# First batch of a four-batch transformer kernel: a second set of buffers for every other chunk, and another order of loads and set-up

## The reference, cut to what matters

```python
x = x + attn0(ln(x))   # one head, key and value size 64, causal, biases on q, k, v and the output
x = x + ffn0(ln(x))    # ln(x) and the weight clipped to +-448 and rounded to fp8 e4m3, product in fp16, + bias
x = x + attn1(ln(x))   # 16 heads of size 16, rotary embedding on q and k, causal
x = x + ffn1(ln(x))    # xr, xk mix a row with the row before it; sigmoid(xr Wr) * (relu(xk Wk)^2 Wv)
```

## Time and profile before

| what | us |
|---|---|
| median of 3 runs | 2985.44 |
| lowest and highest | 2980.69 to 2988.47 |
| the profiled execution's own time | 2989.6 |
| its span in the trace | 2987.8 |
| granted TensorE clock, mean over the span | 0.953 |
| PE busy in the span | 2646.4 (89%) |
| DVE, ACT, POOL busy | 2008.9, 1570.6, 400.0 |

### The profile page before, as it was taken

One profiled execution on the slowest core, in us unless ns is written; L12 is line 12 of the kernel. 1 busy time (PEld: TensorE's weight loads), 2 busy tenths in 40 slices (PEclk: granted clock), 3 DMA queues, 4 the chain that ended last, 5 costly groups with the idle time before them and its releaser, 6 DMA issues.

```text
span 2987.8 us, 57907 instructions
## 1 busy us (share of the span) xinstructions
PE 2646.4 (89%) x21682; PEld 1189.2 (40%) x21682; DVE 2008.9 (67%) x4383; ACT 1570.6 (53%) x3137; POOL 400.0 (13%) x417
## 2 busy tenths in 40 slices
PE   3677869989989999999999989999989999999996
PEld 2333333343434434343344434434334443443344
DVE  3435567778684776867675677777667668778822
ACT  1133325656563565655554555655555556666662
POOL 2212102020200302021010202102020110000011
PEclk8788879999999999999999999999999999999998
DMA  2332123131220313113130221313021131121110
GB/s 53 91 98 79 30 64 86 30 88 35 56 80 29 99 34 93 51 44 93 30 92 29 64 82 44 99 34 98 16 76 53 38 107 33 48 58 28 31 33 30
DMA packets 239508, 176.06 MB, mean 59 GB/s; under 512 B 89793, under 2 KB 238978, under 8 KB 239234
## 3 DMA queue, kind: packets, MB, share of 16 engines
q1 hardware_dynamic: 237376, 170.52, 20.4%
q10 hardware_dynamic: 1858, 1.84, 0.2%
HBM read 87.30 MB, written 84.41 MB: 57 GB/s over the span
## 4 chain that ended last, share of the span: by engine, by line
PE 65%; DVE 12%; ACT 8%; SPq 5%; issue 4%; DMA 3%; POOL 1%; DVEq 1%; POOLq 0%; ACTq 0%
PE psum L1484 14%; PE psum L1465 14%; DVE mx L1205 8%; PE psum L1438 7%; ACT probs L1009 5%; SPq L720 4%; PE psum L1374 4%; PE psum L1406 4%; PE psum L1296 3%; PE psum L1348 2%; DMA rest_dram<-parts 2%; PE psum L1502 2%; PE psum L1425 2%; PE psum L1512 2%; PE psum L1531 2%
## 5 line engine op out<-in xcount | busy, mean ns | idle before, releaser
L1205 DVE TENSOR_REDUCE mx<-psum 128x1 f32<-128x512 f32 (+3 forms) x2560 | 1389.4, 601 | 410.5 <-PE psum L1444 218.1
L1009 ACT ACTIVATE probs<-psum 128x512 f32<-128x512 f32 (+3 forms) x2560 | 1186.4, 539 | 705.7 <-PE psum L1465 437.3
L1465 PE MATMUL psum<-qst,kst 34*128 34x512 bf16 (+7 forms) x5120 | 680.5, 354 | 91.1 <-ACT probs L1009 50.3
L1484 PE MATMUL psum<-probs,vs 128*17 128x512 f32 (+3 forms) x5120 | 604.4, 544 | 0.9 <-ACT probs L1009 0.2
L1438 PE MATMUL psum<-kst,qst 64*128 64x512 bf16 (+3 forms) x2560 | 451.9, 359 | 90.2 <-DVE mx L1205 36.1
L1465 PEld LDWEIGHTS psum<-qst,kst 64*128 64x128 bf16 (+1 forms) x5120 | 198.4, 95 | 448.4 <-ACT probs L1009 177.1
L1438 PEld LDWEIGHTS psum<-kst,qst 64*128 64x128 bf16 x2560 | 131.4, 94 | 486.4 <-DVE mx L1205 178.1
L853 POOL TENSOR_SCALAR vare<-mv 128x4 f32<-128x4 f32 x64 | 14.6, 228 | 1733.1 <-DVE mv L1103 1733.1
L969 ACT ACTIVATE probs<-psum 128x1024 f32<-128x1024 f32 x80 | 74.7, 938 | 153.1 <-PE psum L1354 84.2
L1484 PEld LDWEIGHTS psum<-probs,vs 128*17 128x17 f32 x5120 | 86.4, 96 | 166.1 <-issue 112.2
L1472 PE MATMUL psum<-maskk,identh 64*128 64x128 bf16 x2048 | 147.2, 220 | 0.0
(11 more groups left out here) (129 smaller groups left out, 2575.3 us busy)
## 6 DMA issues: line engine op xcount, KB each, us to landing
main_dram<-parts SPq DMA_DIRECT2D x256, 128.0 KB
rest_dram<-parts SPq DMA_DIRECT2D x128, 128.0 KB
qst<-main_dram SPq DMA_DIRECT2D x128, 128.0 KB, 2.8
kst<-main_dram SPq DMA_DIRECT2D x128, 128.0 KB, 2.8
v_dram<-vst SPq DMA_DIRECT2D x64, 136.0 KB, 4.5
vs<-v_dram SPq DMA_DIRECT2D x64, 136.0 KB, 2.2
xs<-x_in SPq DMA_DIRECT2D x16, 512.0 KB, 4.0
x_dram<-xs SPq DMA_DIRECT2D x16, 512.0 KB, 3.0
```

What stands on the lines that cost most here:

```text
L1009: act.activation(probs[:, HG * (step_no(b, hg, k) % 2) + 2 * pair + odd, 0:cols], bank(PLAN.home["scores", item[:4]][odd], 0, cols), ACT.E ...
L1205: dve.tensor_reduce(mx1[:, n % 2, 2 * g + odd, i % TPC, c:c + 1], bank(PLAN.home["max", item[:5]][odd], 0, width(i, c)), AX.X, ALU.max).th ...
L1465: ins = pe.matmul(two[odd][:, 0:CH - off], kst[rows, kslot, part, pair, keys], qst[rows, qslot, part, pair, off:CH], start=(part == 0), st ...
L1484: ins = pe.matmul(bank(7, off, CH, rows=VW, row=32 * h), vtile[:, h, :], probs[:, HG * (step_no(b, hg, k) % 2) + h, 0:CH - off], start=(kb ...
```

## The change

Chunks of batch 0 with odd q get a set of buffers of their own (`lane` 1). Three parts of it are new or doubled (moments, `nm0`, the `mx0` family), the rest is lent by the tail jobs: `xn3` for `xn`, `attT` for `xnT`, the halves of `gate` for `qd` and `xqT`, `xrk` for `roped`. `shared(b, q)` is the chunk that had the same set before; it takes the place of `before(b, q)` in the waits for buffers, in the planner's list and in the engines. For batch 0 it is the chunk two back; chunk (1, 0) follows (0, 2), and from (1, 1) on all is as before. The first tail job waits for the last odd chunk's use of the lent buffers. Chunks still share `osb0`, `probs0`, `tmp16`, `parts`, `rcos`, PSUM and the bank of `values0`, in the order of chunks.

x of chunk (0, 0) becomes SP's first load, x of (0, 1) follows the fp8 weight, and `bf`, `cos` and `sin` come last with semaphores of their own; ACT's two small loads move ahead of its seven. The waits for weights move to the first user. The bias product on PE goes to the first `turnmax0`, the preparation of the fp8 weight on DVE behind the first `turnmax0 d`, the scaling of two later weights behind the second. The clearing of `kst` goes behind the second `root`. Some of the planner's assumed durations change for all batches.

```diff
+def lane(b, q):
+    return q % 2 if b == 0 else 0
+
+def shared(b, q):
+    if b == 0:
+        return before(b, q, 2) if q >= 2 else None
+    return (0, NQ - 2) if (b, q) == (1, 0) else before(b, q)
...
-        add("DVE", "stats", (ln, *c), key(), 2.3, *after, ("norm", p and (ln, *p)), ("root", p and (ln, *p)))
+        add("DVE", "stats", (ln, *c), key(), 1.9, *after, ("norm", same and (ln, *same)), ("root", same and (ln, *same)))
...
-    add("SP", "load x", c, key() - 60.0, 0.1, ("store x2", p2), ("norm", p2 and (2, *p2)), lat=4.0)
+    add("SP", "load x", c, key() - (60.0 if b else 1e4), 0.1, ("store x2", p2), ("norm", p2 and (2, *p2)), lat=4.0)
...
-    add("SP", "rows0", c, key(), 0.2, ("turnmax0 d", c), lat=2.5)
+    add("SP", "rows0", c, key(), 0.2, ("turnmax0 d", c), ("rows0", p), last, lat=2.9)
...
-        add("DVE", "rope", (*c, t), key(0.5), 1.7, ("QK1", (*c, t)), ("roped", old),
-            *[("RT", p and (*p, bl)) for bl in range(4)], free=("QK1", (*c, t)))
+        add("DVE", "rope", (*c, t), key(0.5), 1.45, ("QK1", (*c, t)), ("roped", old),
+            *[("RT", same and (*same, bl)) for bl in range(4)], ("rope", p and (*p, t)), free=("QK1", (*c, t)))
...
-        add("DVE", "nmax", me, end, 0.9, *[("max d", (*unit, odd)) for unit in units for odd in range(2)], ("turnmax", old))
+        add("DVE", "nmax", me, end, 0.7, *[("max d", (*unit, odd)) for unit in units for odd in range(2)], ("turnmax", old))
...
-        add("DVE", "out", me, end + 2, 1.05, ("turnout", me), ("put att", block_before(b, hg, q, 2)),
+        add("DVE", "out", me, end + 2, 0.8, ("turnout", me), ("put att", block_before(b, hg, q, 2)),
...
+        xns, xnTs, qds = (xn, xn3), (xnT, attT), (qd, gate[:, 0, :])
+        xqTs = (xqT, gate[:, 1, 0:CH // 2].bitcast(FP8).rearrange("p (c n) -> p c n", c=DC))
+        ropeds = (roped, xrk[:, :, :, :].rearrange("p i c n -> p (i c) n"))
...
+            load_x(0, 0)
             for dst, src in [(wqk0[:, :, s, twin, :], cw(w["wqk0"])[:, :, DK0 * s:DK0 * (s + 1)])
...
+            sp.dma_start(raw, cw(w["wf"])).then_inc(S["weights f"], 16)
+            load_x(0, 1)
+            sp.dma_start(bf[:, :], w["bf"].rearrange("(a d) -> a d", a=1).broadcast_to([P, D])
+                         ).then_inc(S["weights f"], 16)
+            sp.dma_start(cos[:, :, :], w["cos"].rearrange("(t p) d -> p t d", p=P)).then_inc(S["weights r"], 16)
+            sp.dma_start(sin[:, :, :], w["sin"].rearrange("(t p) d -> p t d", p=P)).then_inc(S["weights r"], 16)
...
-                    if item == (0, 0, 0):
+                    if item == (0, 0, 1):
                         pool.memset(kst[:, :, 1, :, :], 1.0).then_inc(done, 1)
...
+                    if item == (0, 0):
+                        wt.wait_ge("apart", 1)
+                        wt.wait_ge("weights", W0)
+                        dve.tensor_tensor(wo0[DK0:DK0 + 1, 0:D], bank(7, 0, D, rows=1, row=DK0),
+                                          wo0[DK0:DK0 + 1, 0:D], ALU.add).then_inc(S["ready"], 1)
+                        eight_bit_weights()
+                    elif item == (0, 1):
+                        later_weights()
```

More of the change, by code:

```diff
@@ L242, in chunk_jobs @@
     c = (b, q)
-    p, p2 = before(b, q), before(b, q, 2)
+    p, p2, same = before(b, q), before(b, q, 2), shared(b, q)
     add = o.add
     def norm(ln, *after):
-        add("DVE", "stats", (ln, *c), key(), 2.3, *after, ("norm", p and (ln, *p)), ("root", p and (ln, *p)))
-        add("POOL", "root", (ln, *c), key(), 1.4, ("stats", (ln, *c)), ("norm", p and (ln, *p)))
-        old = (2, *p) if ln == 0 and p else (ln - 1, *c) if ln else None
+        add("DVE", "stats", (ln, *c), key(), 1.9, *after, ("norm", same and (ln, *same)), ("root", same and (ln, *same)))
+        add("POOL", "root", (ln, *c), key(), 1.4, ("stats", (ln, *c)), ("norm", same and (ln, *same)))
+        old = (2, *same) if ln == 0 and same else (ln - 1, *c) if ln else None
         add("DVE", "norm", (ln, *c), key(), 1.2, ("root", (ln, *c)),
@@ L322, in chunk_jobs @@
         old = (*CHUNKS[n // 4], n % 4) if n >= 0 else None
-        add("PE", "RT", (*c, bl), key(), 0.43, *[("roped", (*c, t)) for t in range(TPC)], ("put", old), lat=0.1,
+        add("PE", "RT", (*c, bl), key(), 0.43, ("RT", p and (*p, bl)), *[("roped", (*c, t)) for t in range(TPC)], ("put", old), lat=0.1,
             claim="P", mode="F")
@@ L418, in both @@
         return (("turned", (ln, *c)),)
-    turn("A", ("load att", c), *[("V", p and (*p, n)) for n in range(2)])
+    lent = (0, NQ - 1) if c == (0, 0) else None
+    turn("A", ("load att", c), *[("V", p and (*p, n)) for n in range(2)],
+         *[("QK1", lent and (*lent, t)) for t in range(TPC)], *[("V1", lent and (*lent, n)) for n in range(2)])
     for n in range(2):
@@ L436, in tail_jobs @@
         add("PE", "R", (*c, n), key(), 1.71, ("mix", (*c, 0)), lat=0.1, claim="P", mode="F")
-        add("ACT", "gate", (*c, n), key(), 0.6, ("R", (*c, n)), ("addv", p and (*p, n)), free=("R", (*c, n)))
+        add("ACT", "gate", (*c, n), key(), 0.6, ("R", (*c, n)), ("addv", p and (*p, n)),
+            lent and (("FFN", lent) if n else ("scores0", (*lent, TPC * NQ // 2 - 1))), free=("R", (*c, n)))
     for n in range(2):
@@ L926, in _ @@
                     ln, b, q = item
-                    old = before(b, q)
+                    at = lane(b, q)
+                    old = before(b, q) if ln in ("A", 3) else shared(b, q)
                     wt.job("turn", item)
@@ L954, in _ @@
                     b, q, side = item
-                    old = before(b, q)
+                    old = shared(b, q)
+                    wt.wait_ge("weights", W0)
                     wt.job("scores0", old and (*old, TPC * (old[1] + 1) // 2 - 1))
                     wt.job("QK0", item)
-                    dst = kd[:, CH * q:CH * (q + 1)] if side else qd[:, :]
-                    act.activation(dst, home("QK0", item), ACT.Identity, bias=bqk0[:, side:side + 1]
+                    dst = kd[:, CH * q:CH * (q + 1)] if side else qds[lane(b, q)]
+                    act.activation(dst[:, :], home("QK0", item), ACT.Identity, bias=bqk0[:, side:side + 1]
                                    ).then_inc(S["qk0"], 1)
@@ L1084, in _ @@
                     ln, b, q = item
-                    old = before(b, q)
+                    old = shared(b, q) if ln < 3 else before(b, q)
+                    at = moments(ln, b, q)
                     wt.job("norm", old and (ln, *old))
@@ L1127, in _ @@
                     q = i // TPC
-                    wt.job("nmax0", before(b, q))
+                    wt.job("nmax0", shared(b, q))
+                    mx = mx0[:, lane(b, q), :, :]
                     wt.job("max0", item)
@@ L1172, in _ @@
                     b, q, t = item
-                    old = before(b, q)
+                    old = shared(b, q)
+                    wt.wait_ge("weights r", 32)
                     n = TPC * chunk_no(b, q) + t - 2
@@ L1291, in _ @@
                         wt.job("norm", item)
[L1292 removed]
+                        src = xn3 if ln == 3 else xns[lane(b, q)]
                     two = two_banks(kind, item)
```

202 lines of the change are left out of this document (112 added, 90 removed).

## The result

The changed kernel takes 2911.9 us (median of 4, 2903.1 to 2915.0), the kernel before 2985.1 beside it; the ratio is 0.9748, 95% interval 0.9725 to 0.9770. So it is 73 us faster. 88 were forecast, and the time lies inside the range.

The account below looks back on a forecast made before the run. The chain through one chunk was taken to set the pace from 34 to 450 us, and PE to bound the kernel after that. Terms of 19 + 59 + 10 = 88 us gave 2898 us against the median, range 2855 to 2950.

Parts of the forecast that it names:

- Term 1, the start: Before the first transposes: set-up leaves the path, so they start near 10.8 us instead of 30.1; 19 us kept.
- the gain reaches the end unchanged: After 450 us: PE binds and waits for nothing else left late, so all 88 us stay to the end.
- what is left in front of the first transposes: Start: x landing, PSUM clearing, statistics, constants, root and normalisation, adding up to transposes near 10.8 us.
- The memset, costed at nothing: Start: kst's clearing, moved behind the second root, can strike chunk 1's normalisation, up to 5.2 us, but is covered; 0.
- Term 2: From 34 to 400 us: two chunks at once turn 366 us into 307, a gain of 59.
- The work bound: From 34 to 400 us: PE's work takes 302 us at 91.8% busy, less 20 for the clock, 282.
- the packing term: From 34 to 400 us: 25 us added because both chunks wait at once at times, about 85% busy instead of 92%.
- The 163 us at 1.2 GHz: Working for the clock gain: slow-clock time added over six windows; at most 60 us comes back, 20 taken.
- the fuller case: Rival: lanes pack as well as later stages and more slow clock comes back; 133 us saved, 2853; chance 0.18.
- The maxima of block 3: The 50 us after 400: with chunk 3 earlier, blocks 1 and 2 cover these maxima; at most 15 us, 10 taken.
- The new durations, costed at 0: After 450 us: reordering all four batches changes nothing, PE's work being the same; bounds 25 us either way.
- The rival of parts and SP's queue: Rival: two lanes double ACT's waits for unlanded parts and queue behind puts; 40 us lost, 48 saved, 2938; chance 0.20.

Follow-up runs that it names:

- Experiment 1: The changed kernel with one set of buffers (lane always 0), new start and new durations kept: 2959.0 us, 0.9919 of the kernel before.
- experiment 2: The kernel before with only the planner's new assumed durations: 2971.1 us, 0.9961 of the kernel before.
- experiment 3: The changed kernel with set-up and loads back at their old places, both sets of buffers kept: 2915.6 us, 0.9771 of the kernel before.
- experiment 5: The changed kernel with four slots of parts in batch 0 instead of two, planner told so: 2896.5 us, 0.9715 of the kernel before.
- experiment 9: The changed kernel with only put's planner times corrected (3.8 and 4.0 us for 0.6 and 3.0), rows0 on a semaphore for each lane: 2807.6 us, 0.9412.
- experiment 6: The changed kernel with all of SP's issue times in the planner as traces show them (put, put v, loads, rows): 2818.1 us, 0.9446.
- experiment 4: The changed kernel with x of chunk 1 as SP's second load instead of its eleventh: 2909.0 us, 0.9753 of the kernel before.

## Why the prediction was right, and where its terms were off

The regime of the first 400 us was read rightly, that of the rest only in part. The chain of one chunk held the first 400 us, a second set of buffers opened it, and nothing after 450 us took the gain back. Experiment 1 shows the first two, because the second set alone is 51 of the 73 us; the marks show the third.

**The sum, read from the traces.** The first copy of transposes comes 14.0 us earlier (19 forecast), the stretch from it to chunk 3 on DRAM is 53.5 us shorter (59), the one from there to the end of block 3 is 3.7 us longer (10 shorter), and the rest up to the last mark is 8.0 us shorter (0): 71.8 in all.

**Term 1, the start: 19 forecast.** With one lane it was right: transposes at 11.35 (10.8) and `QK0` at 14.50 (15.1). Only 12 to 13 us of these 19 are left at the end (experiments 1 and 2), so "the gain reaches the end unchanged" failed for this term. With two lanes the first transposes moved from 30.14 to 17.46, 12.7 us, and what is left is 4 to 7, not resolved (experiment 3). The failed step there is "what is left in front of the first transposes": it took each engine's work and not its order. DVE's list had chunk 1's statistics in front, which waited 7.25 us. The prices of the single steps were right: statistics began at 5.16 (5.4), and with that wait removed the transposes began at 11.36.

**The memset, costed at nothing.** It did strike chunk 1's normalisation, 6.25 us again. But the cover failed: PE's order put chunk 1's transposes ahead of chunk 0's `QK0`, and this waited 5.2 us with its input ready. I had asked what DVE does next, not what PE lists next.

**Term 2, 59 forecast.** SP issues the loads of chunk 3's k at these times, before and after:

```profile
400.20 1.08 SPq L750 DMA_DIRECT2D kst<-main_dram  x1
```

```profile
332.65 0.62 SPq L783 DMA_DIRECT2D kst<-main_dram  x1
```

The first copy was at 33.5 and is at 19.4, so 366.7 us have become 313.2, a gain of 53.5. PE is busy 260.5 us in it, 83.2%, where 85% was assumed, and that is 16.6 us less than the 277.1 before, where 20 was assumed for the clock; the granted clock is 0.91 instead of 0.82. The work bound was the right one to count from and the packing term a little too small. Part of what stood in the way is shown by experiment 5: 27 us of waiting for slots, gone with more slots, and 20 us won. (The 163 us at 1.2 GHz in the working take in 33 that lie behind this stretch, and the fuller case's 2853 lies just outside the range that is said to hold most of it; neither moves the sum.)

**The maxima of block 3, 10 forecast, nothing came.** The lead is 67.5 us at these loads and 63.8 at the end of block 3. The stretch only moved, and grew by 3.7 us. Windows of the changed kernel:

```profile
340.00:360.00 20.00, 17.52 (x160) 8.49 (x158) 16.71 (x32) 6.63 (x18) 0.00 (x0) 0.84 0.07 19
360.00:380.00 20.00, 10.21 (x73) 3.88 (x71) 17.44 (x44) 0.00 (x0) 1.26 (x2) 0.50 0.01 3
380.00:400.00 20.00, 17.51 (x155) 6.23 (x155) 17.42 (x41) 12.15 (x23) 2.35 (x1) 0.91 0.12 35
```

From 360 to 380 us ACT does nothing and DVE 17.4 of 20 us: blocks 1 and 2 were finished by then (block 2's copy is at 357.7), and no scores were left to cover the maxima.

**The new durations, costed at 0 of a range of 25.** They gave 12 us alone (experiment 2). "PE's work there is the same and no order makes it less" was the wrong step, and by more than its size tells: PE's share was 92 to 93% and looked like a full engine, but orders with put's true times took 20 to 22 us more from each of batches 1 and 2 (experiment 9). The work was indeed the same, but the time was not only work. In batches 1 and 2 together PE's idle time fell from 94.6 to 68.3 us and its busy time from 1288.6 to 1272.3; over the whole trace the idle time fell from 284.4 to 213.0 and the busy time from 2628.8 to 2589.1 (page of experiment 9). The clock accounts for the fall of the busy time: PE was busy 163.0 us under a granted clock of 0.5 in the changed kernel and 86.5 in experiment 9, and with half of that taken off what is left is 2547 and 2546 us of work (an estimate from the clock records of the two traces). That the sum came within 15 us owes something to errors of opposite signs, -5, -5.5 and -14 against +8, and so in part to luck.

The rival of parts and SP's queue named the right thing at the wrong place. It was priced as a loss that the second lane brings. The wait was there in all batches before, and the second lane didn't double it: up to 400 us ACT waited 26.5 us for parts where it was 40.1, and in the whole trace 91.2, where it was 104.7 in the kernel before and in experiment 1 alike.

Of the signs that the forecast named, three failed besides the first transposes. Chunk 2's first copy came at 98.1 us (near 85 was named). Chunk 3's norm-2 copy came at 287.8 (260 at the latest), since it took 157.3 us on its way and not 93.8. And the lead grew after block 3. PE was busy 84.1% from 50 to 330 us at a clock of 0.90, just at what was named. PE's share after 450 us stayed at 91 to 93%, which had been named as a sign that the end of the sum holds; it held, and still hid the 94 to 104 us of experiments 6 and 9.

## What to carry to other kernels

When a kernel's orders come from a list scheduler, compare its assumed durations with the trace first, those of the queue that issues DMAs above all: the two times of one job, 0.6 us for six issues that take about 4 and 3.0 instead of 4.0 for the landing, cost more here than the whole change gained. A busy share of 92 to 93% doesn't show that an engine is full: here another order made it 95% at a higher granted clock. And when set-up or a load is moved, walk each engine's list and ask what stands in front, not only what the step needs.

## What was unexpected in the hardware

A 5.2 us memset on GpSimd again stretched four small DVE normalisations to 6.25 us (four without it took 1.35), at its new place as at its old one; where eight of them stood in one row (experiment 4), they took 7.65 us beside a memset of 5.28. The granted clock was 0.50, so 1.2 GHz, from 360 to 380 us, although PE was busy half of that time, while it waited for DVE between maxima; at 88% busy it was 0.91 in the next 20 us. The 1.00 of the window from 0 to 34 us is for the most part no reading: the changed kernel's trace has no clock record before 28.8 us, and the transposes there took 421 ns each, as later ones under a granted 0.5 (421), not as those under 1.0 (273).
